# Expert weights and rows in two scaled fp16 parts, and the first stage's copies in another order

## What is computed

```python
x = x + jnp.tanh(g_xattn[0]) * _L0_xattn_ref(_layernorm(x), ctx_1024, ctx_1024, mask)
x = x + jnp.tanh(g_ffn[0]) * _L0_ffn_ref(_layernorm(x), ...)
x = x + jnp.tanh(g_xattn[1]) * _L1_xattn_ref(_layernorm(x), ctx_1024, ctx_1024, ...)
x = x + jnp.tanh(g_ffn[1]) * _L1_ffn_ref(_layernorm(x), w_gate, w_up, w_down)
```

```python
logits = xt @ gate_w.T + gate_b
top_w, top_i = jax.lax.top_k(jax.nn.softmax(logits), 2)
def expert(w1e, b1e, w3e, b3e, w2e, b2e):
    h = jax.nn.silu(xt @ w1e.T + b1e) * (xt @ w3e.T + b3e)
    return h @ w2e.T + b2e
y = jnp.einsum('etd,te->td', outs, gate_dense)
z = jax.nn.silu(xt @ ws1.T + bs1) * (xt @ ws3.T + bs3) @ ws2.T + bs2
```

## Time and profile before

| | |
|---|---|
| median of 3 runs | 599.09 us (598.11 to 599.60) |
| the profiled execution | 600.13 us |
| its span | 598.1 us (2.03 us lie around it) |
| TensorE busy | 561.8 us, 94% |
| TensorE weight loads | 465.4 us, 78% |
| VectorE busy | 453.4 us, 76% |
| ScalarE busy | 377.1 us, 63% |
| POOL busy | 257.2 us, 43% |
| moved by DMA | 93.15 MB, mean 156 GB/s |
| mean granted TensorE clock | 0.991 |

### The profile page before, as it was taken

One profiled execution on the slowest core, in us unless ns is written; L12 is line 12 of the kernel. 1 busy time (PEld: TensorE's weight loads), 2 busy tenths in 40 slices (PEclk: granted clock), 3 DMA queues, 4 the chain that ended last, 5 costly groups with the idle time before them and its releaser, 6 DMA issues.

```text
span 598.1 us, 12971 instructions
## 1 busy us (share of the span) xinstructions
PE 561.8 (94%) x3950; PEld 465.4 (78%) x3950; DVE 453.4 (76%) x1248; ACT 377.1 (63%) x729; POOL 257.2 (43%) x291
## 2 busy tenths in 40 slices
PE   8988999998978999999999999989899989989997
PEld 7787888886858999999999997866746646656664
DVE  5968888885735787778888883766889799877765
ACT  5766778665624777767777763245574774874743
POOL 3444755555560125545534435667464650410100
PEclk9979999999999999999999999998999999999999
DMA  8324644452236878888997846553022240200000
GB/s 242 111 83 169 212 159 154 137 209 106 89 125 218 311 236 259 276 270 243 290 284 247 275 146 254 173 205 90 18 86 72 82 147 37 71 1 36 37 36 36
DMA packets 47973, 93.15 MB, mean 156 GB/s; under 512 B 6990, under 2 KB 17306, under 8 KB 47778
## 3 DMA queue, kind: packets, MB, share of 16 engines
q1 hardware_dynamic: 39740, 74.34, 37.0%
q0 software_dynamic: 7440, 17.97, 10.0%
q10 hardware_dynamic: 726, 0.02, 0.1%
HBM read 61.32 MB, written 32.17 MB: 156 GB/s over the span
## 4 chain that ended last, share of the span: by engine, by line
PE 66%; DVE 16%; issue 5%; ACT 5%; another core or an unknown queue 3%; POOL 3%; DMA 2%; SPq 1%; ACTq 0%; DVEq 0%; POOLq 0%
PE bank L1379 12%; PE bank L1381 12%; PE bank L1380 12%; PE bank L1890 10%; PE bank L1311 4%; PE bank L1912 3%; PE bank L1914 3%; DVE xa L2460 3%; PE bank L1853 2%; PE bank L1842 2%; DVE st L2469 2%; DVE sl L2542 1%; PE bank L1365 1%; POOL yr L765 1%
## 5 line engine op out<-in xcount | busy, mean ns | idle before, releaser
L717 POOL TENSOR_TENSOR yg<-yg,b 128x512 f32<-128x512 f32 x31 | 47.5, 1531 | 94.2 <-ACT yg L857 94.2
L669 POOL DMA_INDIRECT rows_by_expert<-n,pos x64 | 64.3, 1005 | 54.3 <-DVE pos L2192 37.8
L765 POOL DMA_INDIRECT yr<-expert_out,out_row x64 | 65.9, 1030 | 29.9 <-issue 19.0
L1890 PE MATMUL bank<-m4Th,wint 128*128 128x512 f16 x192 | 69.0, 380 | 6.4 <-DVE sl L2542 5.7
L1379 PE MATMUL bank<-xTh,wph 128*128 128x256 f32 x248 | 72.3, 291 | 0.3 <-issue 0.2
L1381 PE MATMUL bank<-xTh,wpl 128*128 128x256 f32 x248 | 70.1, 283 | 0.0
L1380 PE MATMUL bank<-xTl,wph 128*128 128x256 f32 x248 | 70.0, 282 | 0.0
L1890 PE MATMUL bank<-m4Tl,wint 128*128 128x512 f16 x192 | 68.8, 379 | 0.0
L2362 DVE TENSOR_TENSOR wpl<-wraw,wph 128x1024 fp32r<-128x1024 f32 x40 | 48.9, 1223 | 11.6 <-ACT wph L857 11.6
L857 ACT ACTIVATE wph<-wraw 128x1024 fp32r<-128x1024 f32 x40 | 42.4, 1059 | 13.6 <-PE bank L1381 8.4
L1379 PEld LDWEIGHTS bank<-xTh,wph 128*128 128x128 f32 x248 | 47.2, 190 | 0.6 <-issue 0.6
(11 more groups left out here) (357 smaller groups left out, 1737.3 us busy)
## 6 DMA issues: line engine op xcount, KB each, us to landing
wraw<-in_wexp SPq DMA_DIRECT2D x40, 512.0 KB
xg<-rows_by_expert SPq DMA_DIRECT2D x31, 256.0 KB, 4.1
expert_out<-yg SPq DMA_DIRECT2D x31, 256.0 KB, 3.1
x_shared<-x SPq DMA_DIRECT2D x8, 512.0 KB
xa<-x_shared SPq DMA_DIRECT2D x4, 1024.0 KB
out<-ost SPq DMA_DIRECT2D x8, 512.0 KB, 2.8
xin<-in_x SPq DMA_DIRECT2D x7, 512.0 KB, 4.0
stage<-in_wexp SPq DMA_DIRECT2D x8, 256.0 KB
```

What stands on the lines that cost most here:

```text
L669: pool.indirect_dma_start(out=xs, out_offset=bass.IndirectOffsetOnAxis(ap=pos[p][:, k, j:j + 1], axis=0), in_=n2[p][:, j, :], in_offset=No ...
L717: pool.tensor_tensor(yg[u % 3], yg[u % 3], b2[:, bass.ds(e, 1), :].broadcast_to([P, 2, D]), ALU.add)\
L765: pool.indirect_dma_start(out=yr[:, c, k, j, :], out_offset=None, in_=ys, in_offset=bass.IndirectOffsetOnAxis(ap=out_row[:, b * GB + c, k, ...
L1890: last = mm(bank[:, at + w, :], wt[:, k, m * P:(m + 1) * P], part[c][:, k, :], start=(q == 0 and k == 0), stop=(q == 1 and k == KD - 1))
```

## The change

It has four parts.

1. In the expert loop the first layer's operands wph, wpl, xTh and xTl are fp16. The rows are scaled by 2^11, each expert's weights by a power of two from their mean square; ScalarE multiplies by `unscale` in the silu and in hTh, VectorE in hTl and in a single's hb, as a scalar that is read from a table at the expert's place. VectorE's subtractions become scalar_tensor_tensor. hTh, hTl and the second layer stay fp32r.
2. There are four buffers wraw, three of wph and wpl. The weights are split for u + 3 instead of u + 2 (on ScalarE ahead of the silu where the unit is a single), and loaded for u + 5 instead of u + 4.
3. For the scales, SP loads each expert's first-layer weights once more in the first stage (`load_early`, 512 KB a step, twice that in step 6), ScalarE squares and sums them (`sum_squares`, one 128x1024 a step, two in step 7), TensorE sums over the partitions (`mean_squares`), and VectorE makes the tables (`weight_scales`) between `routed` and rrow of the last block.
4. The order of the steps: x's transposes go to bank 6, one half behind `probs_t`, one behind the gate; their copies stand ahead of silu(f, 1) and behind the copy of the logits; probsT is copied at the end of the step before; `down(f, 0, 2)` stands ahead of `rank(f)`; n2 has three buffers, and LN2 waits for the scatters of three steps before; POOL computes rstd of g + 1 ahead of the last two scatters.

Line numbers shift: L857 is L888 in the changed kernel, L920 is L951, L874 L905, L950 L986, L1311 L1362, L1379 to L1381 L1427 to L1429. The semaphores that were merged and renamed are left out of the diff, which goes from the buffers to SP, POOL, ScalarE, TensorE and VectorE.

```diff
-        wraw = [wa.put(f"wraw{p}", [P, KD, 2 * F], F32) for p in range(3)]
-        wph = [wa.put(f"wph{p}", [P, KD, 2 * F], F32R) for p in range(2)]
-        wpl = [wa.put(f"wpl{p}", [P, KD, 2 * F], F32R) for p in range(2)]
+        wraw = [wa.put(f"wraw{p}", [P, KD, 2 * F], F32) for p in range(4)]
+        wph = [wa.put(f"wph{p}", [P, KD, 2 * F], F16) for p in range(3)]
+        wpl = [wa.put(f"wpl{p}", [P, KD, 2 * F], F16) for p in range(3)]
...
+            def load_early(g):
+                if g > 1:
+                    sp.wait_ge(sem("norm_step"), early_of(g)[0])
+                for e in early_of(g):
+                    src = i["wexp"][e * (3 * P):e * (3 * P) + 2 * P, :].rearrange("(k p) n -> p k n", k=KD)
+                    sp.dma_start(early[:, e % 2], src).then_inc(sem("early_in"), 16)
...
+                if g + 1 < NG:
+                    load_early(g + 1)
                 store_mid(g - 1, 1 - p)
...
 # POOL
-                rstd_second(g)
                 scatter(f, 1 - p, (0,), first)
                 scatter(f, 1 - p, (0,), second)
...
                 scatter(f, 1 - p, (1,), first)
+                if nxt:
+                    rstd_second(g + 1)
                 scatter(f, 1 - p, (1,), second)
...
 # ScalarE
-                if g >= 2:
-                    act.wait_ge(sem(f"scattered{p}"), g // 2 * (2 * GT * 16))
+                if g >= 3:
+                    act.wait_ge(sem(f"scattered{1 - p}"), (g - 1) // 2 * (2 * GT * 16))
...
+            def sum_squares(e):
+                act.wait_ge(sem("early_in"), 16 * (e + 1 if e < NG - 2 else NE))
+                w = early[:, e % 2].rearrange("p k n -> p (k n)")
+                act.activation(w, w, ACT.Square, accum_out=wsq[:, e:e + 1]).then_inc(sem("norm_step"), 1)
...
                 silu(f, 0)
-                if g > 1:
-                    pt_copy(g)
...
+                if nxt and g > 1:
+                    t1_copy(g + 1, ks=(0,))
                 silu(f, 1)
                 hidden_high(f, 0)
                 logit_copy(f)
+                if nxt:
+                    t1_copy(g + 1, ks=(1,) if g > 1 else (0, 1))
+                sum_squares(g - 1)
                 silu(f, 2)
                 hidden_high(f, 1)
-                if nxt:
-                    t1_copy(g + 1, ks=(0,))
-                if nxt:
-                    t1_copy(g + 1, ks=(1,))
+                if g == NG - 1:
+                    sum_squares(g)
                 hidden_high(f, 2)
...
                 expert_high(g)
+                if nxt:
+                    pt_copy(g + 1)
...
             def weights_high(u):
-                act.wait_ge(sem(f"stage_in{u % 3}"), 16 * (EARLY[u % 3] + u // 3 + 1))
-                if u >= 2:
-                    act.wait_ge(sem("hm_done"), u - 1)
-                copy(wph[u % 2], wraw[u % 3]).then_inc(sem("high_done0"), 1)
+                at = tile_slot(u)
+                experts[u] = act.value_load(tile_expert[0:1, at:at + 1], min_val=0, max_val=NE - 1)
+                arrived, before = raw_in(u)
+                act.wait_ge(sem(arrived), 16 * (before + u // 4 + 1))
+                if u >= 3:
+                    act.wait_ge(sem("hm_done"), u - 2)
+                copy(wph[u % 3], wraw[u % 4], scale_of(wscale, experts[u])).then_inc(sem("high_done0"), 1)
...
 # TensorE
+            def mean_squares():
+                pe.wait_ge(sem("norm_step"), NE)
+                mm(bank[:, 6, 32:32 + NE], mean_of, wsq, start=True, stop=True).then_inc(sem("norm_step"), 1)
...
                 up(f, 0)
                 if g > 1:
                     probs_t(g)
+                if nxt and g > 1:
+                    t1(g + 1, xinr[1 - p], (0,))
...
                 gate(f)
+                if nxt:
+                    t1(g + 1, xinr[1 - p], (1,) if g > 1 else (0,))
                 up(f, 2)
+                if g == 1:
+                    t1(2, xinr[1 - p], (1,))
                 gate_back(f)
-                if nxt:
-                    t1(g + 1, xinr[1 - p], (0,))
-                if nxt:
-                    t1(g + 1, xinr[1 - p], (1,))
                 up(f, 3)
                 if nxt:
                     scores(g + 1, bn)
+                down(f, 0, 2)
                 rank(f)
-                down(f, 0, 2)
-                t2(g, p, nxt)
+                if not nxt:
+                    mean_squares()
+                t2(g)
                 down(f, 2, MS)
...
 # VectorE
+            def weight_scales():
+                dve.wait_ge(sem("norm_step"), NE + 1)
+                ts(wpow, bank[:, 6, 32:32 + NE], SMALLEST, None, ALU.max).then_inc(sem("norm_step"), 1)
...
+                dve.reciprocal(unscale, unscale).then_inc(sem("norm_step"), 1)
+                stt(b3c, b13c[:, 2:4, :], ROW_SCALE, wscale.unsqueeze(1).broadcast_to([P, 2, NE]), ALU.mult, ALU.mult)\
+                    .then_inc(sem("norm_step"), 1)
...
-                tt(wpl[u % 2], wraw[u % 3], wph[u % 2], ALU.subtract).then_inc(sem("low_done0"), 1)
+                stt(wpl[u % 3], wraw[u % 4], scale_of(wscale, experts[u]), wph[u % 3], ALU.mult, ALU.subtract)\
+                    .then_inc(sem("low_done0"), 1)
...
-                    tt(hTl[p], hb[p], hTh[p], ALU.subtract).then_inc(sem("hTl_done"), 1)
+                    stt(hTl[p], hb[p], scale_of(unscale, experts[u]), hTh[p], ALU.mult, ALU.subtract).then_inc(sem("hTl_done"), 1)
```

149 lines of the change are left out of this document (93 added, 56 removed).

## The result

The changed kernel takes 604.63 us (602.36 to 609.99, six runs) beside 598.97 (596.74 to 600.05, six runs) for the kernel before: a ratio of 1.0095, with a 95% interval of 1.0054 to 1.0137. It is slower. Forecast were 583.6 us and 578.5 to 592.3. The profiled executions of e5 (593.72 us) and e17 (602.15 us) are among the slowest of those kernels, at a low clock in parts of their first 200 us, so only their stretches are read and not their totals.

A forecast was written before the change was run, and what follows sets the result against it. TensorE's pace was taken to bound the expert loop, with one to two microseconds of waits per step besides. Terms −2.2 −1.2 −3.6 +0.2 −8.7 = −15.5 us took the median from 599.09 to 583.6 us, range 578.5 to 592.3.

The forecast's parts named there:

- Does another engine take over?: Expert loop: VectorE needs 10.3 of a group's 11.2 us, ScalarE less, DMA share becomes 0.96, so TensorE stays the bound.
- rows decide: Expert loop: trace rows, giving fp16 a gain of 8.7 us, were preferred to the skill page's formula, which gives 0.
- fp16 at 0.109 against 0.120 us: Expert loop: first-layer products of 256 columns start closer together; loop term −8.7 us (0 to −10).
- Step 1: First stage: n1T copied earlier removes the scores' 1.64 us wait, and the clock may stay up; −2.2 us (−1.0 to −3.0).
- Step 2: First stage: a third n2 buffer removes LN2's 1.18 us wait for scatters; −1.2 us (0 to −1.2).
- Steps 3 to 6: First stage: earlier probsT and n1T copies remove two TensorE waits, 0.9 us a step; −3.6 us (0 to −4.0).
- rival C: Steps gain little: the Square delays silu(f, 2) or early weights delay the residual; steps 3 to 7 sum to 0; chance 0.14.
- Step 7: Last step of the first stage: 4.53 us idle before the residual stays, mean_squares adds a wait; +0.2 us (−2.5 to +1).
- rival B: Steps 3 to 6 reach TensorE's floor, −1.0 us each, and step 7's idle goes, −2.6; total 580.4; chance 0.14.
- The tail: Routing before the loop: 1.5 us of small VectorE operations for the tables fit 2.47 us of idle; 0 (to +0.5).
- Rival A: The loop gains nothing: 0.120 us isn't due to type, or DMA or VectorE becomes the bound; 592.3 us; chance 0.13.
- D: Slower: VectorE forms fp16 parts with table scalars at half pace, wpl 2.4 us, groups 17.0 us; near 659; chance 0.03.

The follow-up runs named there:

- e5: Changed kernel with weights split two units ahead again, behind the silu for singles too: 586.31 us, 0.9988 of the kernel before.
- e17: Kernel before with a third n2 buffer and the new order of the steps, no fp16, early loads or Squares: 595.78 us, ratio 0.9947.
- e13: Changed kernel with weights split two units ahead up to unit 8, three from there, and POOL's bias addition cut to 8 columns: 590.69 us, 0.9867 of the kernel before.
- e15: As e14, with the first stage's order of the kernel before, third n2 buffer kept: 601.21 us, 1.0025 of the kernel before.
- e16: Kernel before with only a third n2 buffer and its wait added: 597.2 us, ratio 0.9979.
- e11: As e10, with the first stage's order of the kernel before; third n2 buffer, Squares and early loads stay: 603.86 us, 1.0052 of the kernel before.
- e7: Changed kernel with fixed powers of two as immediates, without early loads, Squares, sums or tables of scales: 591.23 us, 1.005 of the kernel before.
- c_after: Changed kernel, unchanged, run again where the kernel before takes 588 us: 595.51 us profiled, ratio 1.0106.
- e4: Changed kernel with the copy probsT back behind the table load and silu(f, 0): 596.41 us, 1.0141 of the kernel before.
- c_before: Kernel before, unchanged, profiled again on the chip used for c_after: 588.53 us profiled, 587.78 in the median of 23 others.
- e10: Changed kernel with the split of u + 3 last in each unit on ScalarE and VectorE: 603.02 us, 1.0032 of the kernel before.
- e14: Changed kernel, split two units ahead up to unit 8, then three; POOL's full bias addition waits until behind wpl: 601.02 us, 1.0028 of the kernel before.
- e1: Changed kernel with POOL's bias addition cut to 8 columns of 256: 586.92 us, 0.9972 of the kernel before.
- e3: Changed kernel with ScalarE's silu ahead of the weight split for singles too: 592.11 us, 1.006 of the kernel before.

## Why the prediction was wrong

**The step that failed is "Does another engine take over?"** I summed VectorE's work, 10.3 us of a group of 11.2, and answered no. The sum held: in e13 VectorE is busy for 34.74 of 40 us, 9.6 of a group of 11.02. Two things lie outside such a sum.

*The duration of wpl was taken from a schedule in which it was always there first.* POOL's addition started inside 35 of the 40 wpl of the kernel before, never ahead of one, and it was POOL's that was stretched. The earlier trace rows give 1223 ns, and the same table had hTl at 911 ns beside 681 for g3l of the same size. A line whose mean stands 34% above its like is a sign that something stretches it, and the timeline shows POOL's addition beside it; I didn't ask. With the new lead and the shorter group wpl took hTl's place. Nor is the sum what matters then, but the place: TensorE had no reserve behind xTl, so a wpl that is 1.0 us late makes some 0.9 us of idle, by which estimate a group takes 11.2 + 0.9 = 12.1; measured were 12.3 to 13.0. The eight small waits are 7.2 us of the 9.9 by which the stretch from unit 15's transposes on is longer than in e13 (110.59 against 100.71); the rest has no row of its own. The Trainium skill, page "GPSIMD Engine Reference", section "1. Specifications", says that GpSimd shares SBUF interfaces with VectorE and contends with VectorE instructions that have two SBUF inputs. The traces agree: wpl and hTl, with two, were stretched, and xTl, with one in PSUM, took its 0.68 us. By this rule a rival "the collision falls on wpl" belonged in the list; I had read past it.

*The third unit of lead was costed at nothing* ("the weights get a fourth raw buffer and a load one unit earlier"). I named nobody who is queued behind the copy. It stands ahead of xTh(2) and hTh(0) on ScalarE and waits for a load that the full DMA queues can't bring sooner. Against "rows decide": rows show what an instruction waits for in its present place; moved forward it waits longer, for the same event.

**What held.** fp16 at 0.109 against 0.120 us: pairs of 4.35, groups of 11.02, and a loop of 160.0 when both losses are taken out, 0.2 from the forecast. That close a hit is partly luck: a pair gained 0.33 us where 24 × 0.011 = 0.26 were forecast and a group 0.8 where 0.6 were, and e13's remaining waits and three groups of 11.3 to 11.7 took the surplus. The scalars from tables: 62 ns on wpl, 64 forecast. The tables in the routing tail: 161.30 to 163.92, with 1.08 us of idle left ahead of rrow.

**Step 1, right in size, half right in its reason.** I put the low clock down to the gap of 1.64 us and said it "may stay up". It did, at 1.00 in all 14 traces with the new order. But e15 and e16 have the old order and the gap, keep 1.00, and are as short as the new order (14.64, 14.65). The 2.3 us are the clock's alone; the wait itself costs nothing, and it doesn't always bring the drop. Why the clock stayed up in those two is open.

**Step 2, right in sum.** 1.15 for 1.2; but e16 (18.44) gives the buffer alone 0.4. The new order isn't needed for the rest: e11 and e15 have the old one and take 17.66 and 17.77. What they have beyond e16 wasn't tried apart.

**Steps 3 to 6: rival C's sign, not its mechanism.** The Square fitted and the early loads were hidden: e7, without both, takes 70.70 us for these steps and c_after 70.52. The term failed at both TensorE waits "lose their cause. [...] I take 0.9 each". The wait moved in part to ScalarE: probsT now waits there for the transposes with a table load behind it, and in step 5 TensorE's waits fell by only 0.3 us. I priced removed waits on the waiting engine and didn't ask what the copy, moved forward, would itself wait for: the same fault as in the loop. But by e4 this copy still gains some 0.4 us a step, so it doesn't explain why the cycle stayed at 18.38; what took the rest is open. In c_after against c_before steps 5 and 6 were shorter by 0.5 and 0.3 and steps 3 and 4 longer by 0.4 and 0.2.

**Step 7: rival B's part of it was right, for the step.** The new order makes this step shorter in every pair of traces: by 1.1 us in the result, 0.2 in c_after, 3.1 (e10 against e11), 1.3 (e14 against e15) and 3.2 (e17 against e16). I left the idle of 4.53 us in place because I couldn't name its cause; it hung on the order. Which part of the order wasn't tried. The gain doesn't always reach the loop: from n2Tl of block 6 to the loop the same pairs differ by +0.6, +2.5, −2.0, −1.2 and +1.7 us.

**The tail, costed at 0.** In the result 1.4 of the 1.7 us lie ahead of the last rrow, which comes 11.29 us after n2Tl of block 7 instead of 9.93: n2Tl moved forward in step 7 and the routing behind it didn't. In c_after 0.7 of the 2.7 us lie there, and the rest is largely on SP: the eight stores of zero rows took 9.79 us instead of 8.45 (in the result 12.32 and 12.35, no difference), and the first wph came 25.9 us after n2Tl of block 7, 23.5 before. Why the stores are slower there was not settled.

**Rival A** (the loop gains nothing, or DMA or VectorE takes the bound) came nearest. It was given 0.13 and a price of 0 for the loop; a loss inside the loop was in no case but D, whose mechanism (half pace by type) did not occur: undisturbed, wpl takes 1.28 us and xTl 0.68. The sign that the prediction gave for D, a loop over 170 us and wpl above 2, was seen all the same, so it didn't tell half pace from a collision; the mean of wpl, 1546 ns, and its spread did.

## What to carry to other kernels

A duration read from a trace includes its neighbours: before making an engine's reserve smaller, look for operations of the same form with different means, and ask whether two engines' operations with two SBUF inputs can be made to miss each other. An instruction moved forward in a queue takes its wait with it, to stand in front of everything it overtook; find what it waits for, and when that comes. And where a loop's TensorE work is cut, test the cut with the suspected neighbour removed: one shortened operation (e1, e13) showed in a run what three reorderings (e3, e10, e14) could not.
